# Five pieces of a recurrent scan's side work in other places, x transposed ahead of the initial state, and the even bank's bias first

## The chip, the cores and the metric

The kernel runs on one core of a Trainium2 chip. The metric is the device time of one execution in microseconds (us). The engines are named as the profile names them: PE (TensorE; PEld its weight loads), ACT (ScalarE), DVE (VectorE), POOL (GpSimd) and SP (SyncE, which here only issues DMAs).

## The reference

Two blocks are computed over x of 8 batches x 256 time steps x 128 features, in float32. The first is a recurrent cell scanned over time, the second a transformer block in a curved space, conditioned on `cond`.

```python
def step(h, xt):                       # 256 times, h starts as cond (8 x 128)
    m = concat([xt, h]) @ weight + bias          # 256 x 256
    c = tanh(m[:, 128:]); g = sigmoid(m[:, :128] + 1.0)
    h = g * h + (1 - g) * c
x = x + all h
# block 2, per token: layer norm of logmap0(x), scale and shift by cond @ w_ada,
# q, k, v projections (128 x 384), 16 heads of 8, attention over 256 tokens,
# output projection, Moebius addition, a second norm, an MLP 128-512-128, Moebius addition
x = x + block2(x, cond)
```

## The kernel before

**The scan.** All eight batches are columns and the 128 features are partitions. One step t is a loop through three engines. `z_part` on PE (line 830) adds the recurrent product to PSUM, where the part from x and the bias lie already. `tanhs` on ACT (line 1316) takes the gates from there into `sets`. `scan` on DVE (line 1626) makes the new h as one TENSOR_TENSOR_SCAN instruction. So that PE needn't wait for the exact h, a step is computed twice: a guess (from a float16 copy, `guessed`) goes ahead, and the exact value follows with the small difference `rest` (line 1645). In the trace the start of the instruction `state<-sets` of line 1626 marks step t; there are 256. Line 1647 copies h for the next step.

**The side work.** All else that can be done during the scan is cut into pieces that each engine issues between its instructions of the scan. Each engine has generators (`prepare`, `tokens`, `attention`, and `tail` for the end), and `run` lets each go one `yield` further after each step of that engine. The counter `now[0]` is the step number, the *tick*; `at_ticks(now, n)` yields until tick n. On DVE alone there is a half tick as well (t - 0.5), which lies between the copy of h and the guess of step t + 1; `whole(now)` yields on to the next whole tick. So each engine's instructions stand in a fixed order, written by the numbers of tables such as `TOK`, and each engine takes its instructions strictly in that order: one that waits holds up the scan's instructions behind it.

**Tokens.** The 256 steps are four chunks of 64 (`CH`). When a chunk c is through the scan, its tokens go through norm, modulation and q, k, v during the next chunk: `tok_base(c)` is 64 (c + 1), and `TOK` gives ticks from there. For c = 0, 1, 2 this is within the scan, at bases 64, 128 and 192; chunk 3 comes after the scan by another table, `TOK_LAST`. The chain that matters here, with ticks of `TOK` as they are before:

- `xna` 21: ACT normalises four tiles of 128 tokens, one each tick (line 1377), and tells of the second and the fourth by `tok_xn`.
- `modulate` 23 to 26: DVE multiplies and adds two tiles at a time (lines 1788 and 1793 for tiles 2, 3; lines 1798 and 1803 for tiles 0, 1).
- `usq` 25 to 28: ACT squares the four tiles (line 1384). The last raises `tok_usq`, on which POOL at `clip` 29 makes a clipping factor (lines 640 to 646) and raises `tok_clip`.
- `utrans` 26, 27: PE transposes two tiles each tick (line 774).
- `uevac` 29: ACT copies the transposed tiles from PSUM (line 1402) and raises `tok_uT`.
- `qkv` 29 to 36: PE multiplies by the weights, half a tile each tick (line 964). The first half of each tile waits for `tok_uT`.
- `yevac` 31, 33, 35, 37: DVE takes the products, scaled by the clipping factor (line 1813).
- `factor` 42 and `hfac` 49: DVE makes the head factors by iterations on `hy`; the last two instructions are lines 1923 and 1925, with a wait between.

**Preparation.** `prepare` on PE also adds x and the bias for the chunks to come (`x_part`, line 810, 12 ticks for each chunk) and at ticks 74 to 76 makes the products of the shift (lines 913 and 915). ACT takes these at 77, and DVE at tick 79 makes two row sums of 8 rows (lines 1700 and 1702), which SP stores and loads again for the end.

**The start.** ACT's queue issues the DMAs of x's first chunk and of `cond`. PE waits for `cond`, transposes it (line 774), then transposes the first x (four 128 x 128). ACT makes copies of h0 from the first, then copies x for the first 16 steps (`copy_first_xT`, line 1305) and for the other 48. Even steps below 16 have one PSUM bank and odd ones another; `first_x_part(par, k)` adds x (line 793) and then the two halves of the bias (line 796) to one of four pieces. PE issues both even pieces, the guess of step 0, and the two odd pieces around the exact part of step 0.

Of the kernel before, what the change touches and what calls it, by code (L numbers as in the profile page):

```python
# [10 lines left out]
ALU = mybir.AluOpType  # L11
ACT = mybir.ActivationFunctionType
# [7 lines left out]
NB = 8  # L20
STEPS = 256
CH = 64
FIRST = 16
# [48 lines left out]
def tok_base(c):  # L72
# [4 lines left out]
    transpose=1, resid=5, moments=7, norm=10, artanh=12, rho=19, xn=21, modulate=23, utrans=26,  # L77
    uevac=29, usq=(25, 27), clip=29, qkv=(29, 30, 31, 32, 33, 34, 35, 36), yevac=(31, 33, 35,
# [134 lines left out]
def ugrnn_block_kernel(nc, x, cond, w0, b0, wq, bq, wk, bk, wv, bv, wo, bo, wf1, bf1, wf2, bf2, wada,  # L213
                       bada, out):
    ctx = ExitStack()
    with ctx:
# [554 lines left out]
        def _(pe):  # L771
# [16 lines left out]

            def first_x_part(par, k):

                n = NB * FIRST // 2
                z = z_cols(par)[0][:, 256 * k:256 * k + n]
                pe.matmul(z, w0s[:, k, :], view(xT[:, NB * par:NB * par + 1], [2 * NB, FIRST // 2], [1, NB]),
                          start=(k == 0), stop=False, skip_group_check=True)
                for half in range(2):
                    pe.matmul(z, b0h[:, half, k, :], onesh[:, 0:n], start=False, stop=False,
                              skip_group_check=True)
# [24 lines left out]
            pe.wait_ge(consts, 1)  # L822
            pe.wait_ge(load_cond, 16)
            transpose(tb[:, 0, 0:NB], condr[:, :], identf).then_inc(condT_ps, 1)
            for _ in x_transposes(0):
                pass
# [14 lines left out]
            pe.wait_ge(x_split, 1)  # L841
            pe.wait_ge(xT_first, 1)
            first_x_part(0, 0)
            first_x_part(0, 1)
            z_high(0)
            first_x_part(1, 0)
# [13 lines left out]
            def prepare(now):  # L860
# [34 lines left out]
                for k in range(4):  # L895
# [20 lines left out]
                    .then_inc(shift_ps, 1)  # L916
                for c in range(2, NC):
                    yield from at_ticks(now, CH * (c - 1) + 8)
                    yield from x_part(c)
# [355 lines left out]
        def _(act):  # L1275
# [7 lines left out]
            for slot in range(2):  # L1283
                tile_dma(act, x, resid, 0, slot, False).then_inc(load_x0, 16)
            act.dma_start(condr[:, :], cond).then_inc(load_cond, 16)
            act.wait_ge(condT_ps, 1)

            act.activation(copies_of_h(0), view(tb[:, 0, 0:1], [0, 2], [1, NB], [0, 2]), ACT.Copy,
                           scale=2.0).then_inc(condT_sb, 1)
            act.activation(condT[:, :], tb[:, 0, 0:NB], ACT.Copy).then_inc(condT_sb, 1)  # L1290
# [19 lines left out]
            copy_first_xT(0, FIRST).then_inc(xT_first, 1)  # L1310
            copy_first_xT(FIRST, CH).then_inc(xT_sb, 1)
# [52 lines left out]
            def tokens(now):  # L1364
                for c in range(NC):
# [31 lines left out]
                    if c < NC - 1:  # L1397
                        yield
                    squares_of((1,)).then_inc(tok_usq, 1)
# [891 lines left out]
```

## Time and profile before

| | us |
|---|---|
| median of 3 runs | 455.86 (455.79 to 456.7) |
| the profiled execution's own time | 455.24 |
| its span (first to last instruction) | 453.4 |
| first `state` instruction | 10.27 |
| last (256th) `state` instruction | 289.5 |
| PE, DVE, ACT, POOL busy | 343.0, 344.5, 275.8, 71.4 |

The span has three parts: 10.27 us before the first exact step, 279.2 us of scan, and 164 us after it. In a timeline row the first number is the start in us from the span's start, the second the duration, then engine, line, operation, output<-inputs, sizes, and xN for instructions that the row takes together; the bracket is how long the engine had been idle and what ended that. A step's length is the difference of two `state` starts. Steps with nothing beside them take 1.00 us.

### The profile page before, as it was taken

Reading aid. Unit: us, or ns where it says so; the run is one execution under the profiler, and the core shown is the slowest. Engines: PE = TensorE matmul, PEld = TensorE weight load, DVE = VectorE, ACT = ScalarE, POOL = GpSimd, SP = SyncE. Lnnn points to the kernel's source line nnn. Section 1 sums busy time; section 2 is a strip of 40 time slices with the busy share of each in tenths; the row PEclk is TensorE's granted clock in tenths of the full one; section 3 lists DMA queues with packets and bytes.
Section 4 is the critical chain, followed back from the end, with each engine's and each line's share of the span. In section 5 each row is a group of like instructions: output and inputs, shape, how many; then the busy total and the mean of one; then the engine's idle time right before and its main releaser. Section 6 shows DMA issues by size and latency. Waiting matters only on the chain.

```text
span 453.4 us, 11610 instructions
## 1 busy us (share of the span) xinstructions
PE 343.0 (76%) x3768; PEld 215.6 (48%) x3768; DVE 344.5 (76%) x1973; ACT 275.8 (61%) x1031; POOL 71.4 (16%) x146
## 2 busy tenths in 40 slices
PE   4886897787647776647897988979689889767832
PEld 3633664455435454435554555536345446446410
DVE  3889866787999887899987888754932388699883
ACT  2445654455557445557566566646688888954951
POOL 1000000111000111000021000042300215266580
PEclk9999999999999999999999999986679989996958
DMA  6204800020000000000000000000000000000102
GB/s 182 66 1 105 177 2 1 3 48 2 1 1 2 2 0 2 1 2 1 2 1 3 0 4 0 3 2 3 1 2 3 1 3 3 1 3 0 25 1 69
DMA packets 9567, 8.28 MB, mean 18 GB/s; under 512 B 1282, under 2 KB 8212, under 8 KB 9508
## 3 DMA queue, kind: packets, MB, share of 16 engines
q1 hardware_dynamic: 8948, 7.28, 7.0%
q8 instruction: 31, 0.51, 0.4%
q10 hardware_dynamic: 560, 0.27, 0.2%
q14 instruction: 28, 0.23, 0.2%
HBM read 6.47 MB, written 1.08 MB: 17 GB/s over the span
## 4 chain that ended last, share of the span: by engine, by line
DVE 46%; PE 29%; ACT 13%; issue 7%; POOL 2%; DMA 1%; ACTq 0%; DVEq 0%; POOLq 0%
DVE guessed L1626 9%; DVE state L1626 8%; DVE sets L1647 5%; PE zb L830 5%; DVE rest L1645 5%; ACT sets L1316 4%; PE tb L964 3%; PE firsts L1135 3%; PE tb L774 3%; ACT prd L1480 2%; PE zb L1115 2%; ACT prd L1460 2%; PE zb L810 1%; PE firsts L1021 1%; PE tb L935 1%
## 5 line engine op out<-in xcount | busy, mean ns | idle before, releaser
L1316 ACT ACTIVATE sets<-zb 128x32 f32<-128x32 f32 x479 | 106.4, 228 | 110.5 <-PE zb L830 102.4
L830 PE MATMUL zb<-guessed,whh 128*128 128x8 f16 x960 | 64.3, 173 | 24.1 <-DVE guessed L1626 1.3
L1626 DVE TENSOR_TENSOR_SCAN state<-sets 128x32 f32<-128x32 f32 x256 | 57.0, 223 | 27.8 <-ACT sets L1316 25.7
L830 PE MATMUL zb<-rest,whh 128*128 128x8 f16 x480 | 51.5, 178 | 32.8 <-DVE rest L1645 31.7
L830 PEld LDWEIGHTS zb<-rest,whh 128*128 128x128 f16 x480 | 35.5, 112 | 80.5 <-DVE rest L1645 75.1
L1626 DVE TENSOR_TENSOR_SCAN guessed<-sets 128x32 f16<-128x32 f32 x255 | 57.4, 225 | 10.9 <-ACT sets L1316 2.8
L830 PEld LDWEIGHTS zb<-guessed,whh 128*128 128x128 f16 x960 | 44.2, 107 | 42.4 <-DVE guessed L1626 36.2
L1645 DVE TENSOR_TENSOR rest<-state,guessed 128x8 f16<-128x8 f32 x255 | 42.6, 167 | 8.7
L1480 ACT ACTIVATE prd<-zb 128x640 f32<-128x640 f32 x64 | 41.9, 710 | 5.8 <-PE zb L1115 5.1
L1647 DVE COPY sets<-state 128x32 f32<-128x32 f32 x255 | 44.7, 175 | 0.0
L635 POOL TENSOR_TENSOR stat<-mv 128x4 f32<-128x4 f32 x4 | 0.8, 203 | 229.2 <-DVE mv L1779 229.2
L964 PE MATMUL tb<-wqkv,tw 128*128 128x192 f32 x64 | 28.7, 561 | 2.3 <-ACT tw L1402 2.3
L1135 PE MATMUL firsts<-prd,V 128*18 128x64 f32 (+1 forms) x512 | 25.4, 320 | 2.6 <-ACT prd L1480 2.3
L810 PE MATMUL zb<-xT,w0s 128*128 128x128 f32 (+1 forms) x64 | 24.3, 484 | 0.0
L1460 ACT ACTIVATE prd<-firsts 128x512 f32<-128x512 f32 x32 | 19.0, 593 | 7.9 <-PE firsts L1021 7.9
L1115 PE MATMUL zb<-QT,KT 32*128 32x64 f16 (+1 forms) x256 | 18.6, 241 | 5.3 <-ACT prd L1480 5.1
L1021 PE MATMUL firsts<-QT,KT 32*128 32x128 f16 x128 | 17.9, 285 | 3.4 <-ACT prd L1460 3.1
L1135 PEld LDWEIGHTS firsts<-prd,V 128*18 128x18 f32 x512 | 12.5, 101 | 14.5 <-issue 3.1
L1005 PE MATMUL firsts<-prd,V 128*18 128x128 f32 x256 | 19.2, 389 | 0.1
L774 PE MATMUL tb<-identh,qs 128*128 128x128 f16 x128 | 18.2, 295 | 0.5
L964 PEld LDWEIGHTS tb<-wqkv,tw 128*128 128x128 f32 x64 | 15.6, 298 | 2.9 <-ACT tw L1402 2.6
L1956 DVE TENSOR_TENSOR O<-firsts,O 128x512 f32<-128x512 f32 x8 | 5.5, 690 | 14.8 <-PE firsts L1135 14.8
(370 smaller groups left out, 680.9 us busy)
## 6 DMA issues: line engine op xcount, KB each, us to landing
mod<-ada_rows SPq DMA_DIRECT2D x4, 768.0 KB, 11.0
resid<-in_x_dram SPq DMA_DIRECT2D x6, 128.0 KB, 3.0
ffz<-shift_rows SPq DMA_DIRECT2D x4, 131.0 KB, 3.1
out_dram<-state SPq DMA_DIRECT2D x8, 64.0 KB, 2.1
out_dram<-early SPq DMA_DIRECT2D x8, 64.0 KB, 2.1
yy<-in_L_cond_w_ada_dram SPq DMA_DIRECT2D x1, 384.0 KB
early<-in_L_cond_weight_dram SPq DMA_DIRECT2D x2, 128.0 KB
resid<-in_x_dram ACTq DMA_DIRECT2D x2, 128.0 KB, 3.6
```

The lines of the kernel that those rows point to most:

```text
L774: return pe.transpose(dst, src, ident[0:k, 0:k])
L810: pe.matmul(zb[:, c % 2, par, i:i + NB * n], w0s[:, k, :], view(xT[:, NB * t:NB * t + 1], [2 * NB, n], [1, NB]), start=(k == 0 and q == 0) ...
L830: return pe.matmul(bank[:, 256 * k + i:256 * k + i + NB], whh[:, half, k, :], h, start=False, stop=False, skip_group_check=True)
L964: i = pe.matmul(tb[:, j % 2, 192 * n:192 * n + 192], tuT[:, j, :], wqkv[:, 192 * n:192 * n + 192], start=(n == 0), stop=(n == 1), skip_gro ...
L1115: ins = pe.matmul(diag_bank(i)[:, cols], KT[rows, hg, b, kb, :], q_cols(QT[rows, b // 2, hg, :], b, chunks), start=(kb == 1), stop=True, s ...
L1135: ins = pe.matmul(diag_o(b)[VW * hg:VW * hg + VP, out_cols], v_window(b, kb, i, hg), src, start=(g % NI == 0 and kb == 1), stop=False, ski ...
L1316: return act.activation(view(sets[:, n, 3:4], [39, 2], [38, 2], [4, NB]), view(bank[:, i:i + 1], [256, 2], [0, 2], [1, NB]), ACT.Tanh, sca ...
L1460: act.activation(pr[:, g % 4, :], score_bank(), ACT.Exp, scale=SCALE)\
L1480: act.activation(prd[:, g % 3, 2 * half:2 * half + 2, :], zb[:, half, :, 0:QK], ACT.Exp, scale=SCALE)\
L1626: return dve.tensor_tensor_scan(dst, *scan_terms(n), 0.0, ALU.mult, ALU.add)
L1645: dve.tensor_tensor(rest[:, :], view(h_row(t)[:, 3:4], [4, NB]), guessed_h(t), ALU.subtract).then_inc(lo_ready, 1)
L1647: dve.tensor_copy(copies_of_h(0), view(h_row(t)[:, 3:4], [0, 2], [4, NB], [0, 2]))\
```

## The change

- `modulate` goes from tick 23 to 22, `uevac` from 29 to 28. For chunks 0 to 2 the square of the last tile goes behind the copy `uevac`, to tick 29.
- In chunks 0 to 2 the first instruction of `hfac` goes to the half tick 48.5; the second stays at 49, with the wait before it.
- The row sums of the shift go from tick 79, both together, to ticks 84 and 85. PE yields once more before the `x_part` of chunk 2, which so begins at tick 77 and not at 76.
- At the start x is transposed before `cond`, and ACT copies the first 16 steps of x before the copies of h0. The bias has its own function, `first_bias`. For the even bank it comes before x (and carries the flag that starts the bank), for the odd bank both bias pieces stand ahead of the first x piece.

```diff
-    transpose=1, resid=5, moments=7, norm=10, artanh=12, rho=19, xn=21, modulate=23, utrans=26,
-    uevac=29, usq=(25, 27), clip=29, qkv=(29, 30, 31, 32, 33, 34, 35, 36), yevac=(31, 33, 35,
+    transpose=1, resid=5, moments=7, norm=10, artanh=12, rho=19, xn=21, modulate=22, utrans=26,
+    uevac=28, usq=(25, 27), clip=29, qkv=(29, 30, 31, 32, 33, 34, 35, 36), yevac=(31, 33, 35,
...
+            def first_z(par, k):
+
+                return z_cols(par)[0][:, 256 * k:256 * k + NB * FIRST // 2]
+
+            def first_bias(par, k):
+
+                for half in range(2):
+                    pe.matmul(first_z(par, k), b0h[:, half, k, :], onesh[:, 0:NB * FIRST // 2],
+                              start=(k == 0 and half == 0), stop=False, skip_group_check=True)
+
             def first_x_part(par, k):
 
-                n = NB * FIRST // 2
-                z = z_cols(par)[0][:, 256 * k:256 * k + n]
-                pe.matmul(z, w0s[:, k, :], view(xT[:, NB * par:NB * par + 1], [2 * NB, FIRST // 2], [1, NB]),
-                          start=(k == 0), stop=False, skip_group_check=True)
-                for half in range(2):
-                    pe.matmul(z, b0h[:, half, k, :], onesh[:, 0:n], start=False, stop=False,
-                              skip_group_check=True)
+                pe.matmul(first_z(par, k), w0s[:, k, :],
+                          view(xT[:, NB * par:NB * par + 1], [2 * NB, FIRST // 2], [1, NB]),
+                          start=False, stop=False, skip_group_check=True)
...
             pe.wait_ge(consts, 1)
+            for _ in x_transposes(0):
+                pass
             pe.wait_ge(load_cond, 16)
             transpose(tb[:, 0, 0:NB], condr[:, :], identf).then_inc(condT_ps, 1)
-            for _ in x_transposes(0):
-                pass
...
             pe.wait_ge(x_split, 1)
+            for k in range(2):
+                first_bias(0, k)
             pe.wait_ge(xT_first, 1)
-            first_x_part(0, 0)
-            first_x_part(0, 1)
+            for k in range(2):
+                first_x_part(0, k)
             z_high(0)
+            for k in range(2):
+                first_bias(1, k)
             first_x_part(1, 0)
...
                     .then_inc(shift_ps, 1)
+                yield
                 for c in range(2, NC):
...
-            act.wait_ge(condT_ps, 1)
-            act.activation(copies_of_h(0), view(tb[:, 0, 0:1], [0, 2], [1, NB], [0, 2]), ACT.Copy,
-                           scale=2.0).then_inc(condT_sb, 1)
-            act.activation(condT[:, :], tb[:, 0, 0:NB], ACT.Copy).then_inc(condT_sb, 1)
...
             copy_first_xT(0, FIRST).then_inc(xT_first, 1)
+            act.wait_ge(condT_ps, 1)
+            act.activation(copies_of_h(0), view(tb[:, 0, 0:1], [0, 2], [1, NB], [0, 2]), ACT.Copy,
+                           scale=2.0).then_inc(condT_sb, 1)
+            act.activation(condT[:, :], tb[:, 0, 0:NB], ACT.Copy).then_inc(condT_sb, 1)
             copy_first_xT(FIRST, CH).then_inc(xT_sb, 1)
...
                     squares_of((0,))
-                    if c < NC - 1:
-                        yield
-                    squares_of((1,)).then_inc(tok_usq, 1)
+                    if c == NC - 1:
+                        squares_of((1,)).then_inc(tok_usq, 1)
                     yield from at_ticks(now, base + T["uevac"])
                     act.wait_ge(tok_uT_ps, c + 1)
...
                                    ACT.Copy).then_inc(tok_uT, 1)
+                    if c < NC - 1:
+                        yield
+                        squares_of((1,)).then_inc(tok_usq, 1)
...
-                yield from at_ticks(now, 79)
+                yield from at_ticks(now, 84)
...
                                          shift[:, D:D + 1])
+                yield from whole(now)
...
-                yield from at_ticks(now, base + T["hfac"])
+                yield from at_ticks(now, base + T["hfac"] - (0.5 if in_scan else 0))
                 settle(mark)
-                settled(dve.tensor_scalar(ht[:, NH4:NA4], hy[:, NH4:NA4], C_HEAD * M_CLIP, C_HEAD, ALU.mult,
-                                          ALU.min))
+                done_(dve.tensor_scalar(ht[:, NH4:NA4], hy[:, NH4:NA4], C_HEAD * M_CLIP, C_HEAD, ALU.mult,
+                                        ALU.min))
+                if in_scan:
+                    mark = done[0]
+                    yield
+                    settle(mark)
+                else:
+                    settle()
```

## Rows read from the trace of the kernel before

**Rows 1.** The page's costliest groups: count, busy us, mean ns, idle before, what ended it.
```profile
L1316 ACT ACTIVATE sets<-zb 128x32 f32<-128x32 f32 x479 | 106.4, 228 | 110.5 <-PE zb L830 102.4
```

**Rows 2.** Timeline of steps 91 to 96, chunk 0 in its ticks 27 to 32.
```profile
105.24 0.22 DVE L1626 TENSOR_TENSOR_SCAN state<-sets 128x32 f32<-128x32 f32 x1
105.37 0.69 PE L774 MATMUL tb<-identf,tw 128*128 128x128 f32 x2
...
106.40 0.23 DVE L1626 TENSOR_TENSOR_SCAN state<-sets 128x32 f32<-128x32 f32 x1 [0.39 <-ACT sets L1316]
...
107.26 1.04 POOL L641 TENSOR_TENSOR stat<-stat,neg_half 128x4 f32<-128x4 f32 x1
...
107.40 0.23 DVE L1626 TENSOR_TENSOR_SCAN state<-sets 128x32 f32<-128x32 f32 x1 [0.19 <-ACT sets L1316]
...
107.66 0.59 ACT L1402 ACTIVATE tw<-tb 128x512 f32<-128x512 f32 x1
...
108.30 1.01 PE L964 MATMUL tb<-wqkv,tw 128*128 128x192 f32 x2 [0.78 <-ACT tw L1402]
...
109.64 0.23 DVE L1626 TENSOR_TENSOR_SCAN state<-sets 128x32 f32<-128x32 f32 x1 [1.47 <-ACT sets L1316]
...
110.64 0.23 DVE L1626 TENSOR_TENSOR_SCAN state<-sets 128x32 f32<-128x32 f32 x1 [0.22 <-ACT sets L1316]
...
111.93 0.23 DVE L1626 TENSOR_TENSOR_SCAN state<-sets 128x32 f32<-128x32 f32 x1
```

**Rows 3.** Line L1402: who waited for it, us in all, times.
```profile
  PE tb L964: 2.3, 3
```

**Rows 4.** Timeline of step 86: the second normalised tile, and the guess after it.
```profile
100.35 0.48 ACT L1377 ACTIVATE tw<-resid,stat 128x128 f32<-128x128 f32 x1
...
100.68 0.23 DVE L1626 TENSOR_TENSOR_SCAN guessed<-sets 128x32 f16<-128x32 f32 x1
```

**Rows 5.** Timeline of steps 113 and 114, where the head factors end.
```profile
130.21 0.23 DVE L1626 TENSOR_TENSOR_SCAN state<-sets 128x32 f32<-128x32 f32 x1
...
131.36 0.22 DVE L1626 TENSOR_TENSOR_SCAN state<-sets 128x32 f32<-128x32 f32 x1
```

**Rows 6.** Timeline of steps 76, 77, 79 and 80, beside the shift's products.
```profile
89.13 0.23 DVE L1626 TENSOR_TENSOR_SCAN state<-sets 128x32 f32<-128x32 f32 x1 [0.39 <-ACT sets L1316]
...
90.47 0.23 DVE L1626 TENSOR_TENSOR_SCAN state<-sets 128x32 f32<-128x32 f32 x1 [0.21 <-ACT sets L1316]
...
92.55 0.22 DVE L1626 TENSOR_TENSOR_SCAN state<-sets 128x32 f32<-128x32 f32 x1
...
93.91 0.22 DVE L1626 TENSOR_TENSOR_SCAN state<-sets 128x32 f32<-128x32 f32 x1
```

**Rows 7.** Timeline of the start, up to the bias of the first piece.
```profile
5.32 0.24 PE L774 MATMUL tb<-identf,condr 8*128 8x8 f32 x1 [5.32 <-DMA condr<-in_cond_dram]
...
5.49 1.11 PE L774 MATMUL tb<-identf,resid 128*128 128x128 f32 x4
...
6.64 1.10 ACT L1305 ACTIVATE xT<-tb 128x128 f32<-128x128 f32 x2 [0.78 <-PE tb L774]
...
7.18 0.66 PE L793 MATMUL firsts<-xT,w0s 128*128 128x64 f32 x2 [0.58 <-ACT xT L1305]
...
7.77 0.28 PE L796 MATMUL firsts<-onesh,b0h 1*128 1x64 f16 x2
```

**Rows 8.** Instructions on `resid`: duration ns min/median/max, first and last start us.
```profile
L549 ACTq DMA_DIRECT2D resid<-in_x_dram x2: 630/670/710, 0.7 to 1.5; - x2
```

**Rows 9.** DMA issues of ACT's second load of x: KB, us from issue to landing.
```profile
resid<-in_x_dram ACTq DMA_DIRECT2D x1, 128.0 KB, 3.4
```

**Rows 10.** Windows: the part after the scan; us, busy (count) by engine, PEclk, DMA.
```profile
289.50:453.40 163.90, 123.38 (x1580) 71.36 (x1578) 107.77 (x657) 112.68 (x362) 55.36 (x103) 0.85 0.03 8
```

**Rows 11.** Windows of line L1135 alone: us, PE and PEld busy (count), PEclk, DMA.
```profile
354.00:356.50 2.50, 1.48 (x32) 0.74 (x32) 1.00 0.00 0
334.00:335.50 1.50, 1.27 (x16) 0.51 (x16) 0.50 0.00 0
```

## The prediction, made before the change was run

> **What bounds the kernel now.** I read the page first, then the starts of the 256 `state` instructions in the timeline, then the steps that stand out. The page's costliest group is ACT's gate instruction, idle 110.5 us, of which 102.4 end with PE [rows 1]: no engine is full, the scan goes round PE, ACT and DVE, each waiting for the one before. So it is the longest step of the loop that counts, not busy time. A step with nothing in its way takes 1.00 us, and most take 1.00 to 1.10. Anything that an engine issues between two pieces of the scan is free as long as it fits the engine's gap; what doesn't fit lengthens that one step. The clear case is step 93 [rows 2]: `state` at 107.40 and then at 109.64, 2.24 us, DVE idle for 1.47 of it. ACT begins the copy L1402 at 107.66 and takes 0.59; PE's product L964 had been ready 0.78 earlier and begins at 108.30; the exact part of step 94 is queued behind it on PE. Three chunks have this: PE waited for L1402 3 times, 2.3 us [rows 3]. The sum is made against the profiled execution, 455.24 us (span 453.4 and 1.84 around it); the median of the runs, 455.86, is 0.62 above it.
>
> **The copy and the product (steps 93, 157, 221).** The copy now stands one tick earlier. Step 91 ends with `state` 92 at 106.24 (next paragraph); as before the copy starts 0.26 behind `state`, so 106.50, and ends at 107.09. PE gets to the product 107.52 - 107.40 = 0.12 after `state` 93 (108.30 less 0.78), which is now 107.24: so 107.36, and the copy's result is 0.2 early. The wait is gone. What is late next is the product itself: half a tile takes PE about 1.0 us. The same product lies in steps 94 and 95, which take 1.00 and 1.29 [rows 2]: one delays PE's exact part, and the next finds the guess already made and is free. I take 1.29 for step 93, the first of such a pair: 0.95 gained, 2.85 in three chunks. Were it 1.00 it would be 3.7. Against it: the copy must fit ACT's gap, which held a square before. It ends 0.85 behind `state` 92, and the next gate instruction is wanted about 0.27 before `state` 93, at 0.73; instructions on ACT overlap by about a tenth, so the cost is 0 to 0.12 each; I take 0, since step 93 delays `state` anyway.
>
> The square of the last tile goes to tick 93. POOL's power started 0.86 behind `state` of that square's tick (107.26 against 106.40), takes 1.04, and a short one follows: done some 2.3 after `state`, now 107.24 + 2.3 = 109.6. The user is DVE's first `yevac` in tick 95: `state` 95 is at 107.24 + 1.29 + 1.00 = 109.5, and rest, copy and guess come before it, so about 110.2. Hidden, with 0.6 to spare; what is more than 0.6 late would hold DVE, and behind it the scan.
>
> **`modulate` one tick earlier.** Step 91 took 1.16 [rows 2]: the transposes of tiles 0 and 1 begin at 105.37, when DVE's last addition lands, and end at 106.06, in the way of the exact part. That addition is now a tick earlier, the transposes start as soon as PE is through the guess. 0.16 in three chunks, 0.48 (0 if their own 0.69 is what doesn't fit). The price is a new wait: DVE's two multiplications now stand in the same tick as ACT's tile that they need. In step 86 that tile ends at 100.35 + 0.48 = 100.83, and DVE's guess starts at 100.68 and ends at 100.91 [rows 4]; `modulate` could issue at about 100.82 and waits a few hundredths for the semaphore. `state` 87 is queued behind it. Six such places; bounds 0 and the whole tile, 0.48 each; taken near the row, 0.03 each, a loss of 0.2 in all (2.9 at the far end).
>
> **`hfac`.** Step 113 takes 1.15 [rows 5] since two dependent instructions and the wait between them stand in one gap of DVE. The first now lies at the half tick, between the copy of h and a guess that waits for that copy anyway; its wait is over when the second comes. 0.15 in three chunks, 0.45. Bounds: the same as a loss, if the half tick pushes the guess, and 0.45 as a gain.
>
> **The shift.** Step 76 takes 1.34 and step 79 1.36 [rows 6]. In 76 PE has the shift's last product and the first piece of `x_part`; with the piece a tick later it has one of them, as the neighbours have. In 79 DVE has both row sums and two pieces of the logarithm. I take 1.05 for each: 0.29 + 0.31 = 0.60. The row sums come back at 84 and 85, where DVE has only the scan (`modulate` starts at 86): nothing each, at most half of 79's 0.36 each. All twelve pieces of `x_part` move by a tick, to 77 to 88; the same lengths beside the same steps, nothing. SP's stores and loads of the shift go some 5 us later and are read only after the scan. Bounds 0.24 and 0.70.
>
> **The start.** x's second load is issued at 1.5 [rows 8] and lands 3.4 later [rows 9], at 4.9, while PE's first transpose was let go by `cond` at 5.32, and x's began at 5.49 [rows 7]. Now they run from 4.95 to 6.06 instead of to 6.60. ACT's first copy takes 7.18 - 6.64 = 0.54: done at 6.64. Meanwhile PE transposes `cond` (0.17) and does the two even bias pieces (0.22 to 0.28 each), to about 6.75. So x's first piece starts at 6.75 instead of 7.18: 0.43. The two bias pieces (0.44) are gone from the way to the guess of step 0. The odd bank now has both its bias pieces between that guess and the exact part (0.22 more) and none between the exact part and the next guess (0.22 less), which even out at step 1. Together 0.87. The copies of h0 are ready on ACT at 7.0 instead of 5.9 and DVE needs three short instructions: about 7.4, before PE is ready for the guess at 6.75 + 2 x 0.59 = 7.9. Bounds 0.3, if DVE or h0 is late next, and 1.0 (`cond`'s whole 0.54 and the 0.44).
>
> **The sum.** 2.85 + 0.48 - 0.20 + 0.45 + 0.60 + 0.87 = 5.05. After the scan nothing is reordered, so it should come forward as a whole: 455.24 - 5.05 = 450.2 for a profiled execution, and with the 0.62 between it and the median 450.8 us.
>
> **The rivals.**
>
> *The stall comes back elsewhere.* Copy, square or clipping factor is late by some tenths in the new place, or a product that no longer has 1.4 us of stall before it lengthens two steps instead of one. For: gaps are tight, and all three engines lie within 0.2 us of each other there. Against: the slack above. Price 0.5 in each chunk: 450.8 + 1.5 = 452.3.
>
> *POOL holds up DVE.* POOL's power, 1.04, now lies beside running steps, where before most of it lay in the stall. If an instruction of DVE had to wait for the whole of it, each chunk would pay up to 1.04: 450.8 + 3.1 = 453.9. Against: the power of rows 2 runs from 107.26 to 108.30, and the `state` scan in it starts at 107.40, 0.19 of idle that ACT ended, and takes 0.23 like all others. The Trainium skill, page "SBUF — State Buffer", section "Who interferes with whom", says that a DVE instruction with two SBUF inputs and a GpSimd instruction that reads SBUF take an exclusive lock, so the second is blocked until the first is through. The scan has two such inputs. By that rule the time would be this rival's; the row speaks against it, as it shows no block.
>
> *`modulate` waits for real.* If DVE comes to it before ACT's tile as a rule, 0.2 each instead of 0.03: 1 us, 451.8; at the far end 453.5.
>
> *Slower than before: PE's granted clock after the scan.* That part takes 163.9 us at a mean granted 0.85 [rows 10], so some 30% of it is at half clock, the 1.2 GHz level. Sixteen matmuls of L1135 take PE 0.74 us at the full level and 1.27 at the low one [rows 11], and 32 such groups make the chain that the end hangs on. Every group more that falls into a low stretch costs 0.53. Ten more eat the 5.05 and turn the sign; twelve more, 457.2 us. For: nothing in the order says where the low stretches fall, and the later part starts 5 us earlier. Against: the same work in the same order precedes them, and through the whole scan the clock is full.
>
> **Chances.** The forecast 0.80; the stall elsewhere 0.08; POOL 0.04; `modulate` 0.03; the clock 0.03; and 0.02 that several small losses leave no change that a measurement tells (0.2% of the time, 0.9 us, is about what it can tell). From these: faster by over 0.2% 0.95, within it 0.02, slower 0.03. The range 449.3 to 453.2 has at its lower end the copies and products for nothing (3.7 instead of 2.85) and most of the upper bounds, at its upper end the first and third rivals and most of the way to POOL's.
>
> **What would show it.** In the changed kernel's timeline: steps 93, 157 and 221 at 1.0 to 1.3 with L1402 begun a tick before L964, which no longer waits; steps 91, 155, 219 and 113, 177 at 1.00; 76 and 79 at 1.0 to 1.1, and 84, 85 no longer than before; step 86 and 88 within 0.05 of what they were; `state` 0 at about 9.6 and `state` 1 0.87 earlier than before; the last `state` at about 284.4; and 164 us after it. Wrong would be: step 95 long because DVE waits for POOL; step 92 long because ACT's copy doesn't fit; a guess instruction of DVE stretched or late beside POOL's power; a part after the scan more than 1 us off 163.9.

## The result, and the profile after

The changed kernel takes 449.33 us (median of 4 runs, 449.2 to 450.47), the kernel before 456.02 (4 runs, 455.79 to 456.7) in the same comparison: a ratio of 0.9856, 95% interval 0.9837 to 0.9876. Forecast were 450.8 us, a range of 449.3 to 453.2, and faster with a chance of 0.95. The direction and each step's place in the scan came out; the gain was 6.7 and not 5.05. That put the median only 0.03 above the lower end of the range, and one of the four runs, 449.2, lies below it.

The kernel before was executed some 35 times more beside the experiments: one of these, 481.12 us at a mean granted clock of 0.823, fell in a slower state of the chip and is left out everywhere, the others lie between 454.65 and 460.16.

The profiled execution took 449.20 us, its span 447.32. Against the 455.24 before, 6.04 are gone (6.12 of the span). The starts of the `state` instructions say where:

| part of the span | before | after | gained | forecast |
|---|---|---|---|---|
| to `state` 1 | 11.81 | 10.26 | 1.55 | 0.87 |
| `state` 1 to `state` 255 | 277.69 | 273.45 | 4.24 | 4.18 |
| from there to the end | 163.94 | 163.61 | 0.33 | 0 |

Within the scan, step by step (a step is the difference of two `state` starts; those before stand in [rows 2, 5, 6] for chunk 0):

| steps | before | after | forecast |
|---|---|---|---|
| 93, 157, 221 (copy and product) | 2.25, 2.24, 2.25 | 1.27, 1.28, 1.28 | 1.29 |
| 91, 155, 219 (transposes) | 1.16, 1.17, 1.16 | 1.00 | 1.00 |
| 86, 88 (`modulate`) | 1.05, 1.02 | 1.10, 1.09 | 0.03 longer |
| 113, 177, 241 (`hfac`) | 1.15, 1.15, 1.49 | 1.00, 1.00, 1.28 | 0.15 less |
| 76, 79 (shift) | 1.34, 1.36 | 1.04, 1.09 | 1.05 |
| 84, 85 (row sums' new place) | 1.02, 1.05 | 1.02, 1.06 | the same |
| 114 | 1.06 | 1.19 | not foreseen |

The page's row of the gate instruction, to be held against [rows 1]:

```profile
L1326 ACT ACTIVATE sets<-zb 128x32 f32<-128x32 f32 x479 | 106.5, 227 | 106.3 <-PE zb L836 97.1
```

ACT now waits 4.2 us less in all, 5.3 less for PE. The timeline of steps 90 to 95 answers to [rows 2]; lines 1411, 975, 1638 and 1826 are what 1402, 964, 1626 and 1813 were:

```profile
103.15 0.67 PE L774 MATMUL tb<-identf,tw 128*128 128x128 f32 x2
103.19 0.23 DVE L1638 TENSOR_TENSOR_SCAN state<-sets 128x32 f32<-128x32 f32 x1 [0.22 <-ACT sets L1326]
...
104.19 0.22 DVE L1638 TENSOR_TENSOR_SCAN state<-sets 128x32 f32<-128x32 f32 x1 [0.23 <-ACT sets L1326]
...
104.43 0.59 ACT L1411 ACTIVATE tw<-tb 128x512 f32<-128x512 f32 x1
...
105.15 0.99 PE L975 MATMUL tb<-wqkv,tw 128*128 128x192 f32 x2
105.19 0.22 DVE L1638 TENSOR_TENSOR_SCAN state<-sets 128x32 f32<-128x32 f32 x1 [0.23 <-ACT sets L1326]
...
106.21 1.04 POOL L641 TENSOR_TENSOR stat<-stat,neg_half 128x4 f32<-128x4 f32 x1
106.46 0.23 DVE L1638 TENSOR_TENSOR_SCAN state<-sets 128x32 f32<-128x32 f32 x1 [0.49 <-ACT sets L1326]
...
107.34 0.24 POOL L646 TENSOR_SCALAR stat<-stat 128x4 f32<-128x4 f32 x1
...
108.18 0.59 DVE L1826 SCALAR_TENSOR_TENSOR yy<-tb,stat,bqkvb 128x384 f32<-128x384 f32 x1
```

The transposes begin at 103.15 and no longer wait. The copy ends at 105.02, and the product begins at 105.15 without a wait, 0.13 after the copy. (The prediction's own times, 107.09 and 107.36, make 0.27, and not the 0.2 that it states; PE in fact comes to the product 0.04 ahead of `state` 93 and not 0.12 behind it.) POOL's factor is done at 107.58, 0.60 before DVE uses it, the very slack that was forecast. The `state` scan at 106.46 lies within POOL's power and takes 0.23 as ever.

The new wait of `modulate` is in step 86, to be held against [rows 4]:

```profile
98.17 0.48 ACT L1387 ACTIVATE tw<-resid,stat 128x128 f32<-128x128 f32 x1
...
98.55 0.23 DVE L1638 TENSOR_TENSOR_SCAN guessed<-sets 128x32 f16<-128x32 f32 x1
...
98.76 0.43 DVE L1801 TENSOR_TENSOR tw<-tw,mod 128x256 f32<-128x256 f32 x1
```

DVE's multiplication starts 0.21 behind the guess (98.76 - 98.55), and not 0.14 as the one of line 1806 does a tick later (99.65 and 99.79); ACT's tile had ended at 98.65.

The start answers to [rows 7]:

```profile
5.00 1.08 PE L774 MATMUL tb<-identf,resid 128*128 128x128 f32 x4 [5.00 <-DMA resid<-in_x_dram]
...
6.01 0.27 PE L774 MATMUL tb<-identf,condr 8*128 8x8 f32 x1
...
6.12 0.40 ACT L1311 ACTIVATE xT<-tb 128x128 f32<-128x128 f32 x1 [1.87 <-PE tb L774]
6.14 0.37 PE L796 MATMUL firsts<-onesh,b0h 1*128 1x64 f16 x4
...
6.58 1.11 PE L801 MATMUL firsts<-xT,w0s 128*128 128x64 f32 x4
...
7.48 0.29 PE L836 MATMUL firsts<-guessed,whh 128*128 128x8 f16 x4
...
7.71 0.39 PE L796 MATMUL firsts<-onesh,b0h 1*128 1x64 f16 x4
...
8.03 0.69 PE L801 MATMUL firsts<-xT,w0s 128*128 128x64 f32 x2
...
8.51 0.24 PE L836 MATMUL firsts<-rest,whh 128*128 128x8 f16 x2
...
8.61 0.67 PE L801 MATMUL firsts<-xT,w0s 128*128 128x64 f32 x2
...
9.07 0.29 PE L836 MATMUL firsts<-guessed,whh 128*128 128x8 f16 x4
...
10.26 0.23 DVE L1638 TENSOR_TENSOR_SCAN state<-sets 128x32 f32<-128x32 f32 x1 [0.31 <-ACT sets L1326]
```

From the first x piece to the guess it is 0.90, where it was 1.64 before (two times 0.59 and the bias); forecast were 1.18. `state` 0 starts at 9.05, 1.22 earlier than before (10.27), and `state` 1 gains another 0.33. The odd bank's first x piece shows why. In the kernel before a bias pair stood behind it:

```profile
8.95 0.67 PE L793 MATMUL firsts<-xT,w0s 128*128 128x64 f32 x2
...
9.55 0.28 PE L796 MATMUL firsts<-onesh,b0h 1*128 1x64 f16 x2
```

There the next instruction of PE starts 0.60 behind the piece. In the changed kernel a recurrent product follows the odd bank's pieces, and it starts 0.48 behind the first (8.03 to 8.51) and 0.46 behind the second (8.61 to 9.07), though no other x piece lies beside them.

### The profile page after: what moved, and what is told of

Read it like the earlier page. It is cut to its first block, busy times and chain, and to the rows that moved or that the text cites. A ratio compares the mean times of both kernels' runs of the same rounds, so it can differ in the third digit from the quotient of the medians.

```text
span 447.3 us, 11609 instructions
## 1 busy us (share of the span) xinstructions
PE 341.8 (76%) x3768; PEld 215.4 (48%) x3768; DVE 343.7 (77%) x1973; ACT 275.5 (62%) x1031; POOL 71.4 (16%) x146
## 4 chain that ended last, share of the span: by engine, by line
DVE 46%; PE 29%; ACT 12%; issue 7%; POOL 3%; DMA 1%; ACTq 0%; DVEq 0%; POOLq 0%
DVE guessed L1638 8%; DVE state L1638 8%; DVE sets L1659 5%; PE zb L836 5%; DVE rest L1657 5%; ACT sets L1326 4%; PE firsts L1146 3%; PE tb L975 3%; PE tb L774 3%; ACT prd L1492 2%; PE zb L1126 2%; PE firsts L1032 2%; PE zb L816 1%; PE tb L946 1%; ACT prd L1472 1%
## 5 line engine op out<-in xcount | busy, mean ns | idle before, releaser
L816 PEld LDWEIGHTS zb<-xT,w0s 128*128 128x128 f32 x64 | 16.1, 312 | 0.0
```

The costliest lines, as they stand in the source:

```text
L816: pe.matmul(zb[:, c % 2, par, i:i + NB * n], w0s[:, k, :], view(xT[:, NB * t:NB * t + 1], [2 * NB, n], [1, NB]), start=(k == 0 and q == 0) ...
```

## The experiments

In all of them `state` 1 is given from PE's first transpose on, which starts when a load lands: that moment moved between 4.86 and 5.32 us from execution to execution, and x's second load itself landed at 4.72 to 5.14 in the 14 traces. By this count `state` 1 comes at 6.49 before and 5.26 after. The scan is `state` 1 to `state` 255, 277.69 and 273.45. Six executions of the changed order (the changed kernel, e2, e5, e6, e11, e12) lie between 273.36 and 273.66, so that is how far this number can be trusted; a single step repeats within 0.03. e5 to e9 and e11 were executed once each, and are read by their steps, not by their times.

**The start alone, and the five moves alone.** Each half of the change in a kernel of its own:

```diff
 e1_start_only: the kernel before, with x_transposes(0), first_bias, first_x_part and ACT's order of the changed kernel
 e2_five_only: the changed kernel, with the start of the kernel before
```

> The kernel before with the change at the start alone (x transposed first, the bias pieces apart from the x pieces). My theory: the start is a sum of its own, the 1.5 us that the changed kernel is ahead at state 1 come from it alone, and nothing of it is lost or gained later: state 0 at about 9.05, state 1 at about 10.26, every later step as in the kernel before, the scan 1.5 us earlier at its end, time 1.5 to 1.9 us below the kernel before. Rival (part of the gain at the start comes from how the loads of the program fell in that one execution, not from the order): state 1 at 10.8 to 11.0, 0.9 us below before, as predicted blind.

> The changed kernel with the start of the kernel before: the five moves alone. My theory: 4.2 us less than before, all within the scan, by the steps 76, 79, 91, 93, 113 and their like (93, 157, 221 about 0.96 each), and a part after the scan that stays within 0.3 us of 163.9. With the start's 1.5 that adds up to the changed kernel. Rival (the two halves are not additive, as the shorter scan changes what PE's clock does after it): the part after the scan differs by more than 1 us from 163.9.

The start alone: `state` 1 at 5.26, the scan 277.61, 454.27 us, a ratio of 0.9953 (0.9935 to 0.9971). The five moves alone: `state` 1 at 6.50, the scan 273.59, 452.21 us, a ratio of 0.9902 (0.9882 to 0.9921). The two gains add up to 1.23 and 4.1 to 4.2, as in the changed kernel. So the order gives 1.23 of the 1.55 at the start; 0.32 is that in the changed kernel PE is let go at 5.00 by x, and before at 5.32 by `cond`. With `cond` first the part up to that moment was 5.15 to 5.32 in three executions, with x first 4.86 to 5.28 in eleven; the means are 5.25 and 5.07. So about 0.2 of it belongs to the order, and the rest to how the loads landed in these two executions. The rival of e1 (0.9 in all) fell. In e2 the expectation for the part after the scan failed: it was 165.11, over 1 us off, as the rival said. But the rival's reason, the shorter scan, isn't borne out: in e1, whose scan is as long as before, the part is 164.77. More on that below.

**The copy alone.**

```diff
-    uevac=29, usq=(25, 27), clip=29, ...
+    uevac=28, usq=(25, 27), clip=29, ...
...
+                    if c < NC - 1:
+                        yield
+                        squares_of((1,)).then_inc(tok_usq, 1)
```

> The kernel before with one of the moves alone: the copy of the transposed tiles at tick 28 and the square of the last tile behind it at 29, modulate still at 23. My theory: steps 93, 157, 221 fall from 2.24 to 1.27, 2.9 us in all; step 91 stays 1.16 since the transposes still wait for the addition, but they end at 0.8 after state 91, well before the copy is due. Rival (modulate has to go first, or the copy comes too early and waits for the transposes, and holds up ACT's gates behind it): step 92 is lengthened by some tenths and the gain is 2 us or less.

Steps 93, 157, 221 took 1.28, 1.28, 1.29, and no other step differs from the kernel before by as much as 0.05: 2.87 of the scan's 4.24. The time was 453.69 us, a ratio of 0.9943 (0.992 to 0.9967). The move of `modulate` is not needed for it.

**x first, with the bias behind each piece as before.**

```diff
             pe.wait_ge(consts, 1)
+            for _ in x_transposes(0):
+                pass
             pe.wait_ge(load_cond, 16)
```

> The kernel before with x transposed before cond and ACT's copies in that order, but each x piece still followed by its two bias matmuls. Two theories on where the start's 1.54 us come from. Prediction's arithmetic: a pair of bias matmuls costs PE 0.22, and the earlier x gives 0.43; then this gives 0.4 to 0.6 at state 1 and the bias order the rest, 1.0. Theory of the weights: x pieces side by side take 0.45 each instead of 0.59 plus 0.22, as the next weight load runs under the matmul of the piece before, and a pair of bias matmuls in between hinders that; then too the first x piece starts near 6.6 here, state 1 is 0.6 earlier than before, at 11.2, and the pieces stay 0.81 apart. A state 1 at 10.9 or earlier would say that x first does nearly all.

`state` 1 came 6.31 behind the transpose: 0.18 less than before, and at 11.58 in all, 0.23 less. Both theories had named more (0.4 to 0.6); x landed late here, at 5.14, and its transposes began at 5.28. The ratio is 0.9986 (0.9971 to 1.0001), no gain that can be told from none. What the second theory said of the pieces holds: they stay 0.81 apart, and from the first to the guess it is 1.64 again:

```profile
5.28 1.09 PE L774 MATMUL tb<-identf,resid 128*128 128x128 f32 x4 [5.28 <-DMA resid<-in_x_dram]
...
6.95 0.66 PE L793 MATMUL firsts<-xT,w0s 128*128 128x64 f32 x2 [0.39 <-ACT xT L1300]
...
7.54 0.28 PE L796 MATMUL firsts<-onesh,b0h 1*128 1x64 f16 x2
...
7.76 0.69 PE L793 MATMUL firsts<-xT,w0s 128*128 128x64 f32 x2
...
8.59 0.27 PE L830 MATMUL firsts<-guessed,whh 128*128 128x8 f16 x4
```

**The bias behind both x pieces.** This parts two things that the change does at once: it takes the bias from between the x pieces, and it hides the even bias under ACT's copy.

```diff
-            for k in range(2):
-                first_bias(0, k)
             pe.wait_ge(xT_first, 1)
             for k in range(2):
                 first_x_part(0, k)
+            for k in range(2):
+                first_bias(0, k)
             z_high(0)
```

> The changed kernel with the even bank's four bias matmuls moved behind both x pieces and no longer ahead of them, the rest the same. Theory of adjacency (x pieces side by side are cheap, wherever the bias is): the two x pieces still take about 0.90 together, the bias adds its 0.37 behind them, so the guess of step 0 starts 0.3 to 0.4 later than at 7.48, and the bias's cover (PE waiting for ACT's copy) is what is lost; state 1 0.3 to 0.4 later than 10.26. Rival (the bias ahead of x is what makes the x pieces short, say because PE is kept busy while it waits): x pieces at 0.6 each again, the guess 0.7 later or more.

```profile
5.24 1.09 PE L774 MATMUL tb<-identf,resid 128*128 128x128 f32 x4 [5.24 <-DMA resid<-in_x_dram]
...
6.91 1.09 PE L802 MATMUL firsts<-xT,w0s 128*128 128x64 f32 x4 [0.38 <-ACT xT L1312]
...
7.93 0.39 PE L796 MATMUL firsts<-onesh,b0h 1*128 1x64 f16 x4
...
8.25 0.27 PE L837 MATMUL firsts<-guessed,whh 128*128 128x8 f16 x4
```

`state` 1 is at 5.76, 0.50 behind the changed kernel. The guess starts 8.25 - 5.24 = 3.01 behind the transpose, and 7.48 - 5.00 = 2.48 in the changed kernel. The size is between the two theories: 0.32 is the bias itself, and the rest is that the x pieces start 0.09 later and last 0.12 longer (1.02 to what comes next, against 0.90). So the working runs: x first 0.18; the bias no longer between x pieces, even and odd bank together, 6.31 - 5.76 = 0.55; the even bias under ACT's copy 0.50. Sum 1.23.

The theory of adjacency says more than the rows do. What makes an x piece long is a bias matmul directly behind it, and not that its neighbour is another piece: 0.59 to 0.60 to the bias (7.18 to 7.77 in [rows 7], 8.95 to 9.55), but 0.46 and 0.48 to a recurrent product, 0.45 for each of two side by side, and here, where only the second piece has the bias behind it, 1.02 for both. So a bias directly behind a piece costs that piece 0.11 to 0.15, beside the pair's own 0.22. PE's weight load for the bias starts with the bias matmul itself (7.77 and 7.77 in the kernel before), while that for the guess starts at 7.27 in the changed kernel, 0.21 ahead of its product. That fits a load that isn't hidden under the piece, but no run takes it apart.

**Powers on POOL beside the scan.** The rival that the prediction took from the Trainium skill, tried by itself:

```diff
+            settled(pool.memset(powers[:, :], 0.5))
+            pool.wait_ge(h_ready, 20)
+            for _ in range(12):
+                settled(pool.tensor_tensor(powers[:, :], powers[:, :], neg_half[:, 0:4], ALU.pow))
```

> The changed kernel with 12 powers more on POOL, 128x4, each 1.04 us, one behind the other from step 20 on, where the scan has little beside it (steps of 1.00). The result of them is used by nothing. My theory: POOL does not hold up DVE; the steps 20 to 32 stay at 1.00 to 1.02 and no DVE scan starts late. Rival (the lock of the SBUF page: a DVE instruction with two SBUF inputs waits until POOL's is through): the scans wait, each of some 12 steps grows by up to 1 us, 5 to 12 us in all, and by the guess alone at least 0.3 each.

```profile
32.37 4.27 POOL L677 TENSOR_TENSOR powers<-powers,neg_half 128x4 f32<-128x4 f32 x4
33.01 0.17 DVE L1663 TENSOR_TENSOR rest<-state,guessed 128x8 f16<-128x8 f32 x1
...
33.30 0.22 DVE L1644 TENSOR_TENSOR_SCAN guessed<-sets 128x32 f16<-128x32 f32 x1
...
33.74 0.22 DVE L1644 TENSOR_TENSOR_SCAN state<-sets 128x32 f32<-128x32 f32 x1
```

The twelve powers run from 29.04 to 42.08, 1.01 to 1.05 us each. No step of the scan differs by 0.05 from the changed kernel, and the whole is 273.66. Under the four powers of the first row, back to back for 4.27 us, the scans and the subtraction of two SBUF inputs keep their 0.22 and 0.17 and their distance. The lock that the Trainium skill describes ("SBUF — State Buffer", "Who interferes with whom") doesn't show in this case, for these forms: POOL's 128x4 power holds up nothing on DVE. What it would do with larger tensors wasn't tried.

**`modulate` back at tick 23.**

```diff
-    transpose=1, resid=5, moments=7, norm=10, artanh=12, rho=19, xn=21, modulate=22, utrans=26,
+    transpose=1, resid=5, moments=7, norm=10, artanh=12, rho=19, xn=21, modulate=23, utrans=26,
```

> The changed kernel with modulate back at tick 23. My theory: steps 91, 155, 219 return to 1.16 (0.48 more), steps 86, 88 and their like lose the 0.04 to 0.08 that they had grown (0.3 less), so the whole move is worth 0.1 to 0.2 us, not to be seen in a time; steps 93, 157, 221 stay at 1.27. Rival (modulate at 22 is what lets the copy be on time): step 92 or 93 grows too, by 0.1 or more each.

Steps 91, 155, 219 are 1.16 again, 0.48 in all; 86 and 88 fall from 1.10 and 1.09 to 0.99 and 1.01, 87 rises to 1.07; 150 and 152 fall by 0.08 each, 214 by 0.07, 216 by 0.01, together 0.35. By these steps the move is worth 0.13, as expected for this run. The whole scan is 0.28 longer, but equal scans differ by up to 0.3: that this is just the prediction's 0.48 - 0.20 is chance. Step 93 and its like don't change.

**The square left ahead of the copy.**

```diff
+                    if c < NC - 1:
+                        yield
+                    squares_of((1,)).then_inc(tok_usq, 1)
                     yield from at_ticks(now, base + T["uevac"])
                     act.wait_ge(tok_uT_ps, c + 1)
```

> The changed kernel with the last tile's square ahead of the copy, both in ACT's gap of tick 28, as the order was before. My theory: 0.49 and 0.59 don't fit a gap that held one of them, so the copy ends about 0.4 later and the gates of step 93 with it: step 92 grows by 0.3 to 0.4 in three chunks, and part of it is given back in step 93 since the product of tick 93 is then the second of a pair; 0.3 to 1.1 us more in all. Rival (ACT's idle time covers both): step 92 at 1.00 to 1.05, no difference, and moving the square was not needed.

```profile
104.08 0.23 DVE L1636 TENSOR_TENSOR_SCAN state<-sets 128x32 f32<-128x32 f32 x1 [0.23 <-ACT sets L1326]
...
104.31 0.30 ACT L1394 ACTIVATE scr_a<-tw 128x128 f32<-128x128 f32 x1
...
104.60 0.59 ACT L1412 ACTIVATE tw<-tb 128x512 f32<-128x512 f32 x1
...
105.08 0.37 ACT L1326 ACTIVATE sets<-zb 128x32 f32<-128x32 f32 x2
...
105.34 0.23 DVE L1636 TENSOR_TENSOR_SCAN state<-sets 128x32 f32<-128x32 f32 x1 [0.48 <-ACT sets L1326]
```

Step 92 takes 1.26 and not 1.00, in all three chunks; the scan is 0.68 longer. The 0.26 is a little less than the expected 0.3 to 0.4, and step 93 gives back only 0.03 (1.24 here). In the changed kernel the copy alone ended at 105.02 and the next gate started at 104.94, so the two overlap a little and the copy fits to the tenth.

**The square a tick later still.**

```diff
                     if c < NC - 1:
                         yield
+                        yield
                         squares_of((1,)).then_inc(tok_usq, 1)
```

> The changed kernel with the last tile's square one tick later still, at 30. In the changed kernel POOL's factor is done at 107.58 and DVE's first use of it starts at 108.18, 0.6 of slack. My theory: the factor is done about 1.25 later (step 93 lasts 1.27), some 0.7 after DVE comes to it, and DVE waits in tick 95 with the scan behind it: step 95 and its like grow by 0.5 to 0.7, 1.5 to 2.1 in all. Rival (the wait is taken up by the steps after it, which are long for other reasons, 1.26 each with PE as the last): step 95 grows by less than 0.3, and the sum over 95 to 100 by less than 0.2.

```profile
108.29 0.24 POOL L646 TENSOR_SCALAR stat<-stat 128x4 f32<-128x4 f32 x1
108.65 0.62 DVE L1827 SCALAR_TENSOR_TENSOR yy<-tb,stat,bqkvb 128x384 f32<-128x384 f32 x1 [0.45 <-POOL stat L646]
```

Steps 95, 159, 223 take 1.77, 1.73, 1.74 instead of 1.26 or 1.27, the scan 1.34 more. The growth in each chunk, 0.47 to 0.51, is at or just under the low end of what was expected. The slack is real: one tick later, and DVE waits for POOL with the scan behind it.

**The first tile's product in thirds.**

```diff
-    uevac=28, ..., qkv=(29, 30, 31, 32, 33, 34, 35, 36), ...
+    uevac=28, ..., qkv=(29, 30, 32, 33, 34, 35, 36, 37), ...        (and all that follows a tick later)
+                            if j == 0 and T is TOK:
+                                for q in (0,) if n == 0 else (1, 2):
+                                    i = pe.matmul(tb[:, 0, D * q:D * q + D], tuT[:, j, :],
+                                                  wqkv[:, D * q:D * q + D], ...)
```

> The changed kernel with the first tile's product in each chunk of the scan in three pieces of 128 columns over ticks 29 to 31 and not in two of 192, and all that follows a tick later. My theory (a piece is free as long as it fits PE's gap, as the transposes of 0.67 do; one of 0.99 doesn't and costs 0.27 in every second step): steps 93, 94, 95 at 1.00 to 1.03 each, 0.27 less in each chunk, 0.8 us in all, and nothing lost by the shift. Rival (what lengthens the step is the weights' load or the PSUM bank, not the length of the piece): step 93 stays at 1.2 or more, and three pieces cost more than two.

```profile
105.11 0.77 PE L977 MATMUL tb<-wqkv,tw 128*128 128x128 f32 x2
105.16 0.23 DVE L1646 TENSOR_TENSOR_SCAN state<-sets 128x32 f32<-128x32 f32 x1 [0.24 <-ACT sets L1334]
...
106.21 0.23 DVE L1646 TENSOR_TENSOR_SCAN state<-sets 128x32 f32<-128x32 f32 x1 [0.27 <-ACT sets L1334]
```

The first half of the expectation holds: step 93 takes 1.05 instead of 1.27, and of the stretch 93 to 95 0.43 are gone. The second, 0.8 us less and nothing lost by the shift, doesn't: the scan is 273.43, as in the changed kernel. What a chunk had gained is lost behind it: steps 96 to 105 cost 0.25 more, step 124 0.34, and step 132, where three of DVE's value products now share a tick, takes 1.75 instead of 1.29 (against that, step 114 is back at 1.00). The time was 451.65, a ratio of 0.991 (0.9878 to 0.9942); the profiled execution has the longest part after the scan of all, 166.00.

**All the bias ahead of x**, in one execution and then in five more:

```diff
-            for k in range(2):
-                first_bias(0, k)
+            for par in range(2):
+                for k in range(2):
+                    first_bias(par, k)
...
             z_high(0)
-            for k in range(2):
-                first_bias(1, k)
```

> The changed kernel with the odd bank's four bias matmuls ahead of x as well. My theory: PE waits only some 0.06 for ACT's copy after the even bias, so 0.25 to 0.3 of the odd bias's 0.32 delays the x pieces, and 0.32 is gone between the guess and the exact part: the guess of step 0 0.25 later relative to x's landing, state 0 and 1 within 0.1 of the changed kernel's (5.3 between PE's first transpose and state 1). Rival (PE's idle time while the weights of x are loaded swallows the bias): state 1 0.3 earlier.

> The kernel with all eight bias matmuls of the first 16 steps ahead of x, timed. Its one execution had state 1 at 4.96 behind PE's first transpose against 5.26 in the changed kernel, and the same scan. My theory: 0.3 us better than the changed kernel, so about 6.9 us below the kernel before with the same part after the scan, a ratio of 0.985; but that part moves by over 1 us from execution to execution with where PE's low stretches fall, so the interval holds the changed kernel's 0.9856 as well. Rival (the earlier end of the scan falls on a worse place of the clock as a rule): ratio 0.987 or above.

```profile
6.28 0.58 PE L796 MATMUL firsts<-onesh,b0h 1*128 1x64 f16 x8
...
6.79 1.11 PE L801 MATMUL firsts<-xT,w0s 128*128 128x64 f32 x4
...
7.70 0.29 PE L836 MATMUL firsts<-guessed,whh 128*128 128x8 f16 x4
...
8.40 0.19 PE L836 MATMUL firsts<-rest,whh 128*128 128x8 f16 x2
```

`state` 1 comes at 4.96 and 4.97, 0.30 earlier than in the changed kernel: the rival of e11 was right. The first x piece starts only 1.66 behind the transpose instead of 1.58, so four more bias matmuls delay it by 0.08, and from the guess to the exact part it is 0.70 instead of 1.03. The median of five is 450.34 us, a ratio of 0.9862 (0.9818 to 0.9906), between what theory (0.985) and rival (0.987) had named: the 0.3 can be seen in the trace and not in a time.

**The part after the scan.** No experiment was aimed at it, but it is in every trace. Its instructions stand in the same order in all, and its length goes with the place of PE's low stretches. The windows up to the first fall of the clock and through it, in the changed kernel and then in e2 (us, busy of PE, PEld, DVE, ACT, POOL, then the granted clock, DMA):

```profile
283.71:297.10 13.39, 11.22 (x119) 5.38 (x118) 8.67 (x45) 6.08 (x11) 2.15 (x6) 1.00 0.01 2
297.10:307.34 10.24, 9.30 (x139) 5.60 (x140) 2.76 (x6) 6.96 (x24) 5.31 (x10) 0.50 0.01 2
```

```profile
285.23:297.35 12.12, 10.82 (x96) 4.92 (x95) 7.21 (x36) 4.88 (x9) 1.92 (x5) 1.00 0.01 2
297.35:311.00 13.65, 12.06 (x164) 6.72 (x163) 4.56 (x16) 8.35 (x26) 5.38 (x10) 0.50 0.01 2
```

In four of 14 traces (before, after, e4, e5) the clock falls to the low level, 1.2 GHz, 13.4 to 14.0 us after the last `state` and stays for 10.2; there the part takes 163.6 to 164.3. In the other ten it falls after 11.0 to 13.0 and stays for 13.7; there it takes 164.7 to 166.0. The two rows with 0.50 show the two cases. The kernel before and the changed one were both profiled in the short case. No run sets the clock by itself, so this is a match in 14 traces and not a cause shown. The sum of the low stretches doesn't order the lengths: it is 49.9 us in the kernel before and in e12, whose parts take 163.9 and 165.3.

## Why the prediction was right, and where its sizes were off

- *The stall* was read rightly: the copy is 0.13 early at the product (0.27 by the forecast's times), the step is 1.27 (1.29), 2.9 us (2.85). e3 shows it alone, e10 that the rest of the step's length is the product's.
- *Where the square goes* was right in both of its bounds: ahead of the copy it costs 0.26 a chunk (e8), another tick later 0.5 (e9), and the slack was 0.60.
- *`modulate`*: 0.49 gained at the transposes as forecast (0.48), and the new wait costs 0.01 to 0.08 a place and not 0.03, 0.35 in the six places and not 0.20; worth 0.13 by its steps (e7).
- *`hfac`* and *the shift* came at 0.15, 0.15 and 0.21, and at 0.29 and 0.27. Step 114 took 0.12 more: DVE's first multiplication by `hfac` (line 1842) starts 0.30 behind the guess there, where before it was 0.17, and `state` is queued behind it. It is so in every run with the new `hfac` at tick 49, and not in chunks 1 and 2; what the instruction waits for, the traces don't say.
- *The scan as a whole*, 4.24 against 4.18, fits better than its parts: the steps named here make 2.90 + 0.49 - 0.35 + 0.52 + 0.56 - 0.12 = 4.00, and the rest is spread over the other steps, within the 0.3 by which equal scans differ.
- *The start* is the term that was mis-sized: 0.87 forecast, 1.55 measured. Both have two parts. For PE's release by the load, 5.32 to 4.95, the forecast holds 0.37, and 0.32 was measured. For the order 0.50 is left, and 1.23 was measured (e1). So the whole miss is in the order, above all in what the bias costs PE. Three places add it up. First, the x pieces start at 6.58 and not at 6.75, 0.17: the four even bias matmuls take 0.37 together and not twice 0.22 to 0.28, and end before ACT's copy, which was itself done at 6.52 and not at 6.64. Second, between the first x piece and the guess 0.74 are gone and not 0.44 to 0.46, since each pair behind a piece cost 0.22 of its own and some 0.15 of the piece. Third, the odd bank, which was to even out, gains 0.2: guess to exact part is 0.09 longer (0.94 before, 1.03), exact part to the next guess 0.32 shorter (0.88, 0.56). e4 and e5 divide the 1.23: 0.18 for x first, 0.55 for the bias out of the way of the x pieces, 0.50 for the cover under ACT's copy.
- *After the scan* 0 was forecast and 0.33 measured, within what that part moves from one execution to the next in the same case of the clock.
- *From profile to median* I added 0.62 for the kernel before to a profiled 450.2. The changed kernel's median was 0.13 above its profiled execution. Of the 6.69 between the medians 6.04 are in the two traces; the other 0.65 is the choice of executions. The forecast of 450.8 was thus 1.47 too high: 0.68 by the start, 0.06 by the scan, 0.33 by the part after it, and some 0.5 by this step. That the median still lies in the range, by 0.03, is partly luck: the median of the kernel before moved between 455.46 and 456.65 in other comparisons.
- The rivals: POOL holding up DVE is refuted by e6 for instructions of these sizes; the wait of `modulate` stayed under 0.1; the stall came back nowhere. The clock after the scan was priced as ten groups of L1135 more at the low level. In both kernels' traces 52 of that line's 512 matmuls lie in a low stretch, some 3 groups, and in the other twelve 31, 32 or 52; no trace comes near ten more, and the lengths lie at most 2.4 us apart. But not every execution was traced: two of the kernel before took 460.03 and 460.16, at a mean clock of 0.926 instead of 0.933 to 0.947, 3.4 us and more above the median of their comparison, and e3 has an execution of 457.42, 3.7 above its median. One such execution on one side alone moves a comparison by half of the gain, which is why the medians count here, and the traces.

## What to carry to other kernels

In a loop whose engines wait for each other, side work costs nothing up to the width of the gap, and at most all that is above it: compare each piece with the gap it stands in. Here 0.67 on PE, 0.59 on ACT and 0.40 on DVE were free, 0.77 on PE cost 0.05, and 0.99 cost 0.27 in step 93, though almost nothing in step 94 behind it. Move a producer one gap ahead of its consumer on another engine. When you price an instruction of PE that is removed from between two others, price what it did to its neighbour too: here a small bias matmul behind an x piece cost its own time and 0.11 to 0.15 on the piece. And judge changes under 1% by the starts of a marker instruction in the trace, stretch by stretch, since the time of one execution carries load landings and clock phases that aren't the change's.

## What the runs showed of the hardware that was not expected

- Two float32 x pieces (128x64) side by side: 0.90 from the first to the next instruction behind them; with two 1x64 float16 bias matmuls behind each: 1.64. A piece alone: 0.46 or 0.48 to a recurrent product (128x8, float16) behind it, 0.59 or 0.60 to a bias matmul.
- The scan is 273.36 to 273.66 us in the six executions that share it, while the part after it moves by 2.4 us with the place of PE's low stretches: 163.6 to 164.3 when the first lasts 10.2 us, 164.7 to 166.0 when it lasts 13.7.
- Twelve powers of 1.01 to 1.05 us on POOL beside some 13 us of the scan changed no step of it by 0.05.
